# One wide product and two strided copies of a block inversion on GpSimd, and the orders of the steps around them

## What is computed

```python
x = x + 0.5 * ffn(layernorm(x)); x = x + attn(layernorm(x)); x = x + 0.5 * ffn(layernorm(x))
# attn: q, k, v, z from one projection; causal convolution of 4 taps and silu on q, k, v; l2norm of q, k
def step(state, inp):
    qt, kt, vt, gt, bt = inp
    state = state * jnp.exp(gt)[..., None, None]
    pred = jnp.einsum('bhk,bhkv->bhv', kt, state)
    delta = (vt - pred) * bt[..., None]
    state = state + kt[..., None] * delta[..., None, :]
    return state, jnp.einsum('bhk,bhkv->bhv', qt, state)
# then rmsnorm of the output, times silu(z), times W_out
```

## Time and profile before

| | |
|---|---|
| three runs | 3371.46 us median (3368.84 to 3374.24) |
| the profiled execution | 3380.03 us |
| its span | 3378.3 us |
| mean granted clock of TensorE | 0.934 of full speed |
| busy: TensorE, VectorE, ScalarE, GpSimd | 2872.0, 2101.1, 1591.6, 809.3 us |
| attention pipeline | from about 620 to 2850 us |

### The profile page before, as it was taken

How to read it: one execution, slowest core, us unless ns; L and a number is a source line. 1 busy time by engine, 2 the same in 40 slices (tenths; PEclk the granted TensorE clock), 3 DMA queues, 4 the chain that set the end, 5 groups by cost and what they waited for, 6 DMA issues and landing times. The chain is left out here.

```text
span 3378.3 us, 60751 instructions
## 1 busy us (share of the span) xinstructions
PE 2872.0 (85%) x19470; PEld 2089.7 (62%) x19471; DVE 2101.1 (62%) x4327; ACT 1591.6 (47%) x4884; POOL 809.3 (24%) x991
## 2 busy tenths in 40 slices
PE   2699992567999999999999999999998985399993
PEld 2466662234777777777777777777777674266662
DVE  3122223577898898898898898898886544122222
ACT  0111110455766676766766666666765551011110
POOL 3100004342232332332323323323320101300003
PEclk6899995778999999999999999999999996699996
DMA  5122201124434434434434434434433311122212
GB/s 179 41 93 90 90 24 52 64 92 140 150 105 137 144 94 144 137 106 144 125 113 137 137 109 127 149 110 128 138 118 93 96 56 66 59 67 84 93 58 81
DMA packets 361526, 352.18 MB, mean 104 GB/s; under 512 B 213940, under 2 KB 283956, under 8 KB 361268
## 3 DMA queue, kind: packets, MB, share of 16 engines
q1 hardware_dynamic: 346676, 288.00, 27.9%
q0 software_dynamic: 14592, 60.83, 5.1%
HBM read 205.47 MB, written 143.26 MB: 103 GB/s over the span
## 5 line engine op out<-in xcount | busy, mean ns | idle before, releaser
L478 PE MATMUL f_ps_up<-f_wbuf,f_xgT 128*128 x1248 | 499.4, 544 | 5.3 <-issue 3.3
L573 DVE TENSOR_TENSOR f_h<-f_h,f_ps_up 128x448 f32<-128x448 f32 x156 | 96.9, 621 | 555.1 <-ACT f_h L547 555.1
L547 ACT ACTIVATE f_h<-f_ps_up 128x448 f32<-128x448 f32 x156 | 84.8, 544 | 635.2 <-PE f_ps_up L478 635.2
L478 PEld LDWEIGHTS f_ps_up<-f_wbuf,f_xgT 128*128 128x128 f32 x1248 | 231.4, 192 | 189.2 <-issue 184.5
L1437 DVE SCALAR_TENSOR_TENSOR at_vT<-at_bank,at_taps_v,at_vT 128x510 f32<-128x510 f32 (+2 forms) x384 | 280.9, 745 | 75.2 <-ACT at_vT L1310 66.1
L1437 DVE SCALAR_TENSOR_TENSOR at_qk<-at_bank,at_taps_qk,at_qk 128x510 f32<-128x510 f32 (+2 forms) x384 | 284.6, 744 | 50.0 <-ACT at_qk L1303 40.2
L1096 PE MATMUL at_bank<-xnT,at_w_qk 128*128 128x512 f32 x512 | 250.0, 612 | 10.0 <-DMA at_taps_qk<-_L_attn_conv_weight_dram 8.5
L1121 PE MATMUL at_bank<-at_w_vz,xnT 128*128 128x256 f32 x1024 | 243.2, 380 | 13.2 <-DVE at_vT L1437 13.2
L1718 POOL TENSOR_SCALAR at_osum<-at_osum 128x8 f32<-128x8 f32 x64 | 15.1, 237 | 984.4 <-ACT at_junk L1414 984.4
L500 PE MATMUL f_ps_y<-f_wbuf,f_hT 128*128 x1092 | 248.8, 379 | 1.6 <-DVE f_hT L577 1.6
L1109 PE MATMUL at_bank<-xnT,at_w_vz 128*128 128x512 f32 x512 | 235.7, 604 | 14.7 <-DVE at_qk L1437 10.6
(11 more groups left out here) (220 smaller groups left out, 6155.2 us busy)
## 6 DMA issues: line engine op xcount, KB each, us to landing
f_wbuf<-in_L_ffn_w_dram POOLq DMA_DIRECT2D x48, 896.0 KB, 7.9
pt_kept<-at_pt_made SPq DMA_DIRECT2D x64, 512.0 KB, 2.6
mt_kept<-at_mt_made SPq DMA_DIRECT2D x64, 512.0 KB, 4.6
at_mt<-mt_kept SPq DMA_DIRECT2D x64, 512.0 KB, 3.5
at_pt<-pt_kept SPq DMA_DIRECT2D x64, 512.0 KB, 4.3
qk_kept<-at_qk SPq DMA_DIRECT2D x64, 256.0 KB, 3.2
ks_kept<-at_ks_made SPq DMA_DIRECT2D x64, 256.0 KB, 3.3
at_ks<-ks_kept SPq DMA_DIRECT2D x64, 256.0 KB, 4.6
```

Of the source, the lines that this page charges most:

```text
L478: last = te.matmul(ps_up[hf][w][:, 0:MH], xgT[b][:, k, :], wbuf[:, bass.ds(off + (w * WSIZE + k * M + hf * MH), MH)], start=(k == 0), stop ...
L573: v.tensor_tensor(part, part, ps_up[hf][1][:, 0:MH], ALU.mult).then_inc(h_ready, 1)
```

## The change

The product of half (3,0) is issued by GpSimd in a new step `wide`, and its sum stays on VectorE, which waits for it. Half (3,1) is empty; its two copies are a new step `low` on GpSimd, each adding one to `blocks_done`, which now counts two a head. Both steps have stage 5, like `blocks`, and run in the iterations of part 3. The five orders are written anew as well.

```diff
-SP_ORDER = (("blocks_out",), ("load_vz",), ("load_d",), ("load_t",), ("load_c",), ("blocks_in",), ("load_qk",),
-            ("load_wo",), ("spill",))
+SP_ORDER = (("blocks_out",), ("load_c",), ("blocks_in",), ("load_qk",), ("load_wo",), ("load_d",), ("load_vz",),
+            ("load_t",), ("spill",))
 PE_ORDER = (("solve", 0), ("inv_x", 32), ("proj_qk", 0), ("state",), ("inv_n",), ("turn", 1), ("on_state",),
-            ("proj_qk", 1), ("inv_x", 64), ("y_turn",), ("solve", 1), ("turn", 0), ("project", 0), ("project", 1),
+            ("proj_qk", 1), ("inv_x", 64), ("y_turn",), ("solve", 1), ("project", 0), ("turn", 0), ("project", 1),
 ACT_ORDER = (("weigh", 0), ("copy_state",), ("inv_n",), ("turn", 1), ("conv_qk", 0), ("from_state",), ("conv_qk", 1),
-             ("y_copy",), ("norm",), ("weigh", 1), ("turn", 0), ("conv_v", 2), ("conv_v", 3), ("decay_exp",),
-             ("gate_v", 2), ("gate_v", 3), ("gate_qk", 0), ("turn_copies",), ("gate_qk", 1), ("inv_last",),
+             ("y_copy",), ("norm",), ("turn", 0), ("weigh", 1), ("conv_v", 2), ("conv_v", 3), ("decay_exp",),
+             ("gate_v", 2), ("gate_v", 3), ("turn_copies",), ("inv_last",), ("gate_qk", 0), ("gate_qk", 1),
 DVE_ORDER = (("inv_x", 32), ("blocks", 0), ("from_state",), ("conv_qk", 0), ("y_copy",), ("conv_qk", 1), ("inv_n",),
-             ("add",), ("inv_x", 64), ("conv_v", 2), ("conv_v", 3), ("blocks", 1), ("mix",), ("shape",), ("join",))
-POOL_ORDER = (("spread_decay",), ("norm_scale",), ("out_weights",), ("scales",), ("decay_exp",), ("fix_diag",))
+             ("add",), ("inv_x", 64), ("conv_v", 2), ("conv_v", 3), ("shape",), ("mix",), ("blocks", 1), ("join",))
+POOL_ORDER = (("spread_decay",), ("wide",), ("norm_scale",), ("low",), ("scales",), ("decay_exp",), ("fix_diag",),
+              ("out_weights",))
...
-                    at_least(sp, s["blocks_done"], u[0])
+                    at_least(sp, s["blocks_done"], 2 * u[0])
...
                     elif (part, half) == (3, 0):
-                        wide_cols(8, 8, 16)
-                    else:
-                        v_.tensor_copy(w_low[:, 0:16, 0:16], w_up[:, 0:16, 0:16].rearrange("p j i -> p i j"))
-                        v_.tensor_copy(w_low[:, 16:32, 0:16], w_up[:, 0:16, 16:32].rearrange("p j i -> p i j")).then_inc(s["blocks_done"], 1)
+                        n[0] = n[0] + 1
+                        dve.wait_ge(s["block_step"], n[0])
+                        link(v_.tensor_reduce(w_up[:, 0:16, 24:32], triple(0, 16, 8, 16), AX_X, ALU.add, negate=True))
...
+                def wide(u):
+                    if u[1] != BP - 1:
+                        return
+                    pool.wait_ge(s["block_step"], STEPS * u[0] + sum(COUNTS[:6]))
+                    apart()
+                    r_ = half_way[:].rearrange("p (j k) -> p j k", k=16)
+                    g.tensor_tensor(terms[:].rearrange("p (j i k) -> p j i k", i=8, k=16),
+                                    r_.unsqueeze(2).to_broadcast([P, 16, 8, 16]),
+                                    w_low[:, 24:32, 16:32].unsqueeze(1).to_broadcast([P, 16, 8, 16]),
+                                    ALU.mult).then_inc(s["block_step"], 1)
+
+                def low(u):
+                    if u[1] != BP - 1:
+                        return
+                    pool.wait_ge(s["block_step"], STEPS * (u[0] + 1))
+                    apart()
+                    g.tensor_copy(w_low[:, 0:16, 0:16], w_up[:, 0:16, 0:16].rearrange("p j i -> p i j")).then_inc(s["blocks_done"], 1)
+                    g.tensor_copy(w_low[:, 16:32, 0:16], w_up[:, 0:16, 16:32].rearrange("p j i -> p i j")).then_inc(s["blocks_done"], 1)
```

More of the change, by code:

```diff
@@ L788 @@
     "fix_diag": 10, "spill": 10,
-    "blocks_in": 6, "blocks": 5,
+    "blocks_in": 6, "blocks": 5, "wide": 5, "low": 5,
     "blocks_out": 1, "load_c": 1, "load_t": 1,
@@ L1012, in blocks_out @@
                         return
-                    sp.wait_ge(s["blocks_done"], u[0] + 1)
+                    sp.wait_ge(s["blocks_done"], 2 * u[0] + 2)
                     for k, w in enumerate((w_up, w_low)):
@@ L1724, in _ @@
                             "decay_exp": decay_exp, "scales": scales,
-                            "fix_diag": fix_diag, "norm_scale": norm_scale, "out_weights": out_weights})
+                            "fix_diag": fix_diag, "wide": wide, "low": low, "norm_scale": norm_scale, "out_weights": out_weights})
 _INS = ['L0_attn_hidden_states', 'L0_attn_W_qkvz', 'L0_attn_W_ba', 'L0_attn_conv_weight', 'L0_attn_A_log',
```

## The result

| | before | after |
|---|---|---|
| median of six runs each | 3373.8 us (3368.8 to 3375.7) | 3388.9 us (3383.4 to 3395.1) |
| ratio, with its 95% interval | | 1.0047 (1.0034 to 1.0060) |
| the profiled execution, its span | 3380.0, 3378.3 | 3395.1, 3393.4 |
| mean granted clock of TensorE | 0.934 | 0.933 |
| busy: TensorE, VectorE, GpSimd | 2872.0, 2101.1, 809.3 | 2877.1, 2030.0, 887.6 |

The change is slower by 0.47%, 15 us, where I had forecast no change (3370, at most 3384). VectorE lost 71 us of work and GpSimd took 78, and none of the 71 came out of the time. Nearly all of the loss lies ahead of the last `proj_v`: 4.9 us while the pipeline fills, 10.8 over the heads.

A forecast was written before the change was run, and what follows sets the result against it. Steps 1 and 2 were taken as bound by VectorE, step 3 by TensorE, step 4 by a store. Terms -5 + 1 + 2 = -2 us on the profiled 3380.0 gave 3370 on the median, range 3352 to 3384.

The forecast's parts named there:

- The sum: Whole kernel: -5 + 1 + 2 = -2 us on the profiled execution of 3380.0; 3370 on the median.
- Step 3, the wide product: Third of a head's four steps: the GpSimd product takes 3.86 us and stays hidden; cost 0, upper bound 10 us.
- the slack of `y_copy`: Step 3 on VectorE: `y_copy` waited 0.66 us for `y_turn`, so coming 0.4 later would cost 0.
- Step 4, the weights: `load_vz`, issued later, still lands 2 us ahead of use: 0; 13 us should it miss by 1 us.
- signs that I had named for a wrong prediction: In the profile: step 1 under 33, an idle TensorE for `w_vz`, or step 3 over 31.5.
- Step 4, the store: Fourth step of a head: VectorE resumes after the `w_low` store at V + 20.9; -5 us, bounds +5 and -10.
- the wait for the store: Sign of a right forecast: VectorE's 65.6 us waiting for the store gets smaller per head, counted from V.
- Filling: While the pipeline fills: wide product and `low` in the chain (+1), `load_vz` behind the first store (+1); +2 us.
- Steps 1 and 2: First two steps of a head: the new order only moves VectorE's conflict with GpSimd; 0 and +1 us.
- (c): Slower rival: the wide product needs 5 us or the weights come 1 us late; +10 to +13, 3382; chance 0.12.
- (b): Slower rival: more TensorE idling around `solve 1` tips nine more heads to a slow clock; +14, 3384; chance 0.13.
- (a): Faster rival: step 4's store lands as with an empty queue, `y_copy` wait gone; -10 to -12, 3360; chance 0.31.

The follow-up runs named there:

- e15: The kernel before the change, unchanged, profiled again: 3371.6 us.
- e2: The changed kernel with the wide product of (3,0) back on VectorE: 3386.9 us, ratio to before 1.0035.
- e6: The changed kernel with one operand of the GpSimd product read from one address for the 16 innermost elements (true product left out): 3396.6 us, one execution.
- e1: The changed kernel with the load of the v and z weights directly behind `blocks_out` again: 3394.2 us, ratio to before 1.0052.
- e7: The changed kernel with the edits of e1 and e2 together: 3379.3 us, ratio to before 1.0017.
- e9: The kernel before with the copies of (3,1) alone on GpSimd, in the old orders: 3362.6 us, ratio 0.9967.
- e5: The kernel before with one wait more, `spread_decay` on GpSimd starting only after VectorE's `from_state`: 3349.7 us, ratio 0.9934.
- e11: The kernel of e7 with the added wait of e5: 3336.1 us, ratio to before 0.9891.
- e12: The kernel before with the edits of e9 and e5, and VectorE's order changed to `shape`, `mix`, `blocks`: 3333.5 us, ratio to before 0.9879.
- e3: The kernel before with the five new orders alone, product and copies staying on VectorE: 3532.3 us, ratio 1.0471.
- e4: The changed kernel with the five old orders, `wide` behind `spread_decay` and `low` behind `norm_scale`: 3427.7 us, ratio to before 1.0156.

## Why the prediction failed

Point by point, in its own steps.

**The sum.** It said -2 us; measured +15. Means over the executions above, after less before: filling +4.6, the heads +9.6, the rest +1.4. The step from the profiled execution to the median was wrong as well: it put most of 8.6 us down to four slow clock stretches, and e15 has four at 3371.6.

**Step 3, the wide product.** This is the step that failed first: the term 3.86 us for the product on GpSimd, twice a product of 1024. It took 4.51. Its start was well forecast (V + 16.3 worked out, V + 16.35 measured), the rest of the chain too, so the size alone turned the slack of `y_copy` into 0.3 late, 3.6 us over 13 heads. The slack was mis-read too: 0.66 is that of the head shown, 0.5 that of most. e2 (product back) and e6 (3.85 us and step 3 at 30.96) show it from both sides. The Trainium skill (GPSIMD Engine Reference, "3.1 Elementwise — side-by-side cycle accounting") gives 4.50 for two fp32 inputs of 2048 elements; by that rule, this case's 4.51 agrees, and so does the 0.3 a head, 4 us in all, that I had worked out from it. I weighed it as a rival and took the row of another shape of access for the sum; the Trainium skill's figure should have had the forecast. That alone would have moved it by 4 us only.

**Step 4, the weights.** The term 0 ("2 us ahead") failed, and this is the second step: in 13 of 14 heads TensorE starts 0.04 us behind the landing of the last taps, having stood 0 to 1.04 us. e1 prices it: 3.9 us in step 4, and with the filling 7; in the ratios of e2 and e7 it is 6. I had written 13 us for one microsecond too late in each head; in the heads it was 0.3 on the mean. What I had missed in my own working is the transfer's length: the median from issue to landing rose from 3.3 to 4.9 us for the taps and from 4.4 to 5.0 for the weights, and they now go out right behind `load_c`, `load_wo` and `load_d`. That these are what makes them longer was not tested. Of the signs that I had named for a wrong prediction, an idle TensorE for the weights is the one that came true; step 3 stayed under 31.5.

**Step 4, the store.** -5 forecast. With the late weights taken out (e1), step 4 is 415.6 against 415.5: nothing gained. VectorE goes on at V + 21.27 on the mean of 13 heads in both, where I had V + 20.9: from the spill of `pt` it is 7.8 us, not 7.6. `pt` did leave at V + 13.4 as worked out, so what `blocks_in` gave by leaving early the later `mix` took. That the gain was there is shown by e9, where `pt` leaves at V + 11.7 and step 4 drops by 12.0: the mechanism was right, but it belongs to `low` with the old order of VectorE. Of my signs, the wait for the store, 65.6 us in 15 places, is 60.8 in 14: no smaller per head.

**Filling.** +2 forecast, +4.6 measured. e2 and e1 undo 4.5 and 3.5 of it one by one, e7 4.3 on the mean of its two executions, so the two don't add. As executions of before differ by 2.5 us here, the shares of the two are not shown.

**Steps 1 and 2.** "The conflict is moved, not removed" held: the wait of `output` for `mix` is gone, `y_copy` is late in its place (43 times in place of 27), step 2 is 31.97 for 31.86 in each full head and step 1 33.64 for 33.46 apart from slow stretches: 12 x 0.11 = +1.3 and 13 x 0.18 = +2.3, where I had 1 for step 2 and 0 for step 1. e5 shows what the conflict itself was worth, far more than I had thought open to any change of order: 26.2 us in step 1, slow stretches included.

**The rivals.** (c) had both causes right, with a chance of 0.12: the product at 4.5 rather than 5 us *and* the late weights, 11 us in the profile when undone together with the filling. I had joined them with "or", and they came together. (b), the clock: after had 4 and 2 slow stretches, before 4, 3 and 4. The idle time around `solve 1` grew by 0.55 us and did not tip the other nine heads, so the rival as priced is false. A weaker form of it stays open: kernels with the orders of after had 7 (e1), 8 (e6) and 5 and 4 (e7) slow stretches, and three executions of e1 that were not profiled took 9 us more at a clock of 0.931. It is only when the idle stretch of 1.7 goes (to 0.5 in e5, 0.8 in e11 and e12) that the slow stretches vanish: 0 in each of the four runs. (a) is false for the change and true for its half, e9.

**What stays open.** e7, with both causes undone, is 2.9 us over before between first and last `proj_v` and its ratio is 1.0017 (1.0007 to 1.0026). Some 2.6 of the 2.9 are 0.1 us each in steps 1 and 2 of the full heads (33.56 for 33.46, 31.97 for 31.86); which of the new orders does that was not tried by itself. The single terms of after are known no better than the executions agree, some 2 us each for step 4 and the filling. Of the median's 6 us some 3 have no place in the profiles.

## What to carry to other kernels

Moving work from an engine that is not late to a slower one is paid by the shortest slack behind it: write that slack down over all heads (here 0.5 us), and cost the moved instruction by a row with the same kind of operands, not only the same number of elements. Look at where VectorE and GpSimd hold each other up before moving work between them: one wait more on the engine with time to spare gave 23 us here (e5), while the product moved here had cost nothing on VectorE (step 3 is at TensorE's 30.95 in e2). When an order changes in a queue, list who stands behind each waiting entry: the same orders cost 10 us with `low` early (e2) and 156 without it (e3).

## What the runs showed of the hardware

- GpSimd, product of 128x2048 fp32, two operands in SBUF: 4.51 us; with one operand at rest in the innermost index: 3.85 (e6). The latter is twice the 1.93 of 1024 elements, the former isn't.
- A VectorE product of two SBUF operands that falls beside a GpSimd one can stand for the whole of it: 4.62 us for 0.34 in e4, beside a GpSimd product of 4.54. The taps of the convolution (one operand in PSUM) beside `spread_decay` (1.90) take 2.30 for three either way (e5). The Trainium skill (SBUF — State Buffer, "Who interferes with whom") says that a VectorE instruction with at most one SBUF input stays off the shared port; by that rule, the trace agrees.
- Slow stretches of TensorE's clock: 35.1 in place of 33.5 us, in 2 to 8 heads of 14 behind an idle stretch of 1.7 us, on other heads in each execution of the same kernel; in none of the four kernels in which that stretch was 0.5 to 0.9. e4, with 1.75 us in the same place, had one in step 1, and had them in step 3 behind an idle 2.8 (clock 0.95 in the step shown, which took 35.56 us, and 0.91 in those of 36.5 to 36.8).
